# Giving turns and sums the score banks, maxima a ring of their own, and two earlier seams: one core, 32 groups of heads

## The reference: two transformer layers, of which the second layer's cross attention matters most

```python
x = x + _L0_xattn_ref(_layernorm(x), ctx, Wq, bq, Wk, bk)          # softmax over the width
x = x + _L0_ffn_ref(_layernorm(x), gate_w, gate_proj, up_proj, down_proj)   # 8 experts, top 2 of a router
x = x + _L1_xattn_ref(_layernorm(x), ctx, pos, pos, Wq, Wkv, Wout, bout)    # 32 heads of 16, rotary positions
x = x + _L1_ffn_ref(_layernorm(x), Wg, Wu, Wd, Wr, Ag, Bg, Au, Bu, Ad, Bd)

# in _L0_ffn_ref
router_logits = x_flat @ gate_w.T
top_w, sel = jax.lax.top_k(router_logits, TOPK)

# in _L1_xattn_ref
logits = jnp.einsum('bqhd,bkhd->bhqk', q, k) * scale
w = jax.nn.softmax(logits, axis=-1)
attn = jnp.einsum('bhqk,bkhd->bqhd', w, v)
```

## Time and profile before

| what | value |
|---|---|
| median of 3 runs | 1711.52 us (1708.54 to 1712.14) |
| profiled execution: its time, its span | 1712.57 us, 1710.9 us |
| PE, DVE, ACT, POOL busy | 1599.5, 1066.7, 782.0, 457.6 us |
| mean granted TensorE clock | 0.962 |
| router loop | about 160 to 187 us |
| second attention, 32 groups | 645.9 to 1004 us |

### The profile page before, as it was taken

One profiled execution on the slowest core, in us unless ns is written; L12 is line 12 of the kernel. 1 busy time (PEld: TensorE's weight loads), 2 busy tenths in 40 slices (PEclk: granted clock), 3 DMA queues, 4 the chain that ended last, 5 costly groups with the idle time before them and its releaser, 6 DMA issues. The chain is left out here.

```text
span 1710.9 us, 25136 instructions
## 1 busy us (share of the span) xinstructions
PE 1599.5 (93%) x8556; PEld 1173.2 (69%) x8556; DVE 1066.7 (62%) x1959; ACT 782.0 (46%) x1239; POOL 457.6 (27%) x422
## 2 busy tenths in 40 slices
PE   6987789999968989999999989999999999999998
PEld 5776679999957754333333357668888888888886
DVE  5876733222238887999999936655555557545456
ACT  5653323333325526888888853443333333223232
POOL 1120023332227861111210002233233323333332
PEclk8999789999988987999999999989999999999999
DMA  8996126654255764332222212443423345422221
GB/s 276 340 348 243 58 81 225 240 214 151 69 182 181 246 180 111 76 76 76 68 73 69 58 20 98 147 128 130 132 83 133 112 160 228 166 77 77 79 68 50
DMA packets 110364, 236.40 MB, mean 138 GB/s; under 512 B 39888, under 2 KB 53840, under 8 KB 101536
## 3 DMA queue, kind: packets, MB, share of 16 engines
q1 hardware_dynamic: 104000, 214.33, 37.6%
q0 software_dynamic: 6240, 20.45, 3.6%
HBM read 274.84 MB, written 93.45 MB: 215 GB/s over the span
## 5 line engine op out<-in xcount | busy, mean ns | idle before, releaser
L1319 DVE TENSOR_REDUCE early_top<-r_ring 128x1 f32<-128x512 f32 x480 | 304.2, 681 | 16.7 <-PE r_ring L1330 9.2
L2057 ACT ACTIVATE r_probs<-r_st 128x1024 f32<-128x1024 f32 x256 | 251.4, 1023 | 50.6 <-PE r_st L1959 50.3
L48 PE MATMUL f_bank<-late_xnT,late_weights 128*128 128x512 f32 x1056 | 252.4, 391 | 0.0
L48 PEld LDWEIGHTS f_bank<-late_xnT,late_weights 128*128 128x128 f32 x1056 | 196.6, 188 | 41.1 <-issue 0.7
L2855 DVE TENSOR_TENSOR attn<-attn,f_bank 128x512 f32<-128x512 f32 x132 | 90.8, 688 | 195.0 <-PE f_bank L48 130.7
L48 PE MATMUL m_bank<-w_place,m_xT 128*128 x936 | 167.2, 328 | 3.0 <-DVE m_xT L1220 3.0
L2849 ACT ACTIVATE attn<-f_bank 128x512 f32<-128x512 f32 x132 | 78.9, 598 | 179.9 <-PE f_bank L56 125.5
L48 PEld LDWEIGHTS m_bank<-w_place,m_xT 128*128 128x128 f32 x936 | 152.6, 190 | 6.9 <-issue 3.6
L1988 PE MATMUL r_out<-r_probs,early_v 128*17 128x512 f32 x1024 | 136.5, 605 | 0.1
L56 PE MATMUL f_bank<-late_am,late_weights 128*128 128x512 f32 x528 | 135.6, 392 | 0.3 <-DVE attn L2855 0.3
L3060 POOL TENSOR_TENSOR wout_split<-attn,wout_split 128x512 fp32r<-128x512 f32 x66 | 85.6, 1297 | 187.0 <-ACT wout_split L3036 187.0
(11 more groups left out here) (330 smaller groups left out, 2782.3 us busy)
## 6 DMA issues: line engine op xcount, KB each, us to landing
w_place<-expert_split SPq DMA_DIRECT2D x72, 1408.0 KB
w_place<-expert_split SPq DMA_DIRECT2D x36, 1024.0 KB
late_w_dram<-late_weights SPq DMA_DIRECT2D x11, 1920.0 KB, 8.2
expert_split<-w_place SPq DMA_DIRECT2D x10, 1408.0 KB
w_place<-expert_split SPq DMA_DIRECT2D x36, 384.0 KB
late_weights<-late_w_dram SPq DMA_DIRECT2D x11, 1024.0 KB, 5.2
late_weights<-late_w_dram SPq DMA_DIRECT2D x11, 896.0 KB, 4.8
early_slots<-y_rows SPq DMA_DIRECT2D x16, 512.0 KB, 6.5
```

The source lines that it names most:

```text
L48: last = nc.tensor.matmul(out, l, r, start=(i == 0), stop=(i == len(passes) - 1))
L1319: return nc.vector.reduce_max(self.top[g % 2][:, q, h:h + 1], bank[:], AXIS_X)
L2057: nc.scalar.activation(probs[k][:, 2 * pair:2 * pair + 2, :], st_ps[pair][:], ACT.Exp, scale=SCALE).then_inc(exp_done, 1)
```

## The change: who uses which bank, the order of a group, and the work around two seams

1. **Attention banks.** The ring of three holds maxima alone. The two turns go into the first bank of `st_ps[1]` (`turn_ps`). To leave it free for them, scores (1, 1) go into `st_ps[0]`, so that `st_ps[0]` carries five of a group's eight pairs and `st_ps[1]` three.
2. **Order of a group** on TensorE and ScalarE, and VectorE's inversion one maximum later in the group (after the first of q = 3).
3. **Seam into the attention.** The second group's 16 maxima go round seven banks, 12 spare products in place of 8, no wait for the last stores at the block's end (SP and POOL wait later, where the data is used).
4. **Front seam and router.** Statistics, deviation and inverse of tiles 0 to 11 move into the last batch of `phase_attention0`; those of tiles 12 to 15 into the router loop. VectorE normalises three tiles ahead, `xT` has a third place (`third`, in `hT`), the router's weights are turned after tile 1, constants are set behind the loop, and the load of three expert weights waits for tile 10.

```diff
-        PLACES = KT * GROUP + 2
-        SHIFT_PLACE, OUT_PLACE = 4, 8
...
+        turn_ps = st_ps[1][:, 0, :]
+
+        def score_bank(k, pair):
+            return st_ps[0 if (k, pair) == (1, 1) else pair]
+
+        def ring(g, q, h):
+
+            return ring_ps[((g - early.AHEAD) * KT * GROUP + q * GROUP + h) % 3]
...
+            def bank_free(g, q, h):
+
+                wait_count(pe, max_read, (g - AHEAD) * KT * GROUP + q * GROUP + h - 2)
...
-                wait_count(pe, exp_done, (g * KT + k) * 2 + pair - 1)
+                if (k, pair) == (2, 1):
+                    pe.wait_ge(sums_copied, g) if g else pe.wait_ge(shift_copied, 1)
+                else:
+                    wait_count(pe, exp_done, (g * KT + k) * 2 + pair - (0 if (k, pair) in ((1, 1), (2, 0)) else 1))
...
                 wait_count(pe, shift_made, g + 1 - AHEAD)
-                bank_free(g + 1, SHIFT_PLACE)
-                early.turn_shift(nc, g, ring(SHIFT_PLACE), ident).then_inc(shift_turned, 1)
+                pe.wait_ge(exp_done, 2 * KT * (g - 1) + 2)
+                early.turn_shift(nc, g, turn_ps, ident).then_inc(shift_turned, 1)
...
                 pe.wait_ge(out_copied, g + 1)
-                bank_free(g + 3, OUT_PLACE)
+                if g + 2 < GROUPS:
+                    pe.wait_ge(shift_copied, g + 2)
...
-            first_maxima(12, 8)
+            first_maxima(12, 5)
             turn_first_shift()
-            first_maxima(20, 12)
-            spare_products(nc, 8, qk_ps[0][1], wv[:, HI, 0, 0:P], wv[:, HI, 1, :])
+            first_maxima(17, 15)
+            pe.wait_ge(shift_copied, 1)
+            spare_products(nc, 12, shift_ps, wv[:, HI, 0, 0:P], wv[:, HI, 1, :])
...
-            for i in range(RING):
-                sp.wait_ge(qk_out[i], STORES * DMA * len(range(i, PAIRS, RING)))
...
+            for i in range(3):
+                normed_rows(i)
+            for i in range(TILES):
+                lo_x(i)
...
+                if i == 2:
+                    token_moments(nc, n, range(TILES - TPB, TILES))
+                    token_var(nc, n, LATE_TILES)
+                if i == TPB + 2:
+                    token_rstd(nc, dve, n, LATE_TILES, 2)
+                if i + 3 < TILES:
+                    normed_rows(i + 3)
```

More of the change, by code:

```diff
@@ L583, in _ @@
                     prep(b, 3 + t)
+                    if not ahead and t == TPB - 2:
+                        token_std(nc, act, norm, EARLY_TILES, 1)
         @block.vector
@@ L680, in _ @@
                 for t in range(1, TPB):
+                    if not ahead:
+                        token_moments(nc, norm, range((t - 1) * TPB, t * TPB))
+                        if t == TPB - 1:
+                            token_var(nc, norm, EARLY_TILES)
                     add(b, t)
@@ L872, in _ @@
             sp.dma_start(gw_raw, io["L0_ffn_gate_w"]).then_inc(gw_in, DMA)
-            for unit in range(3 * (E0 - 1), weights.UNITS):
-                weights.load(sp, unit)
             for i in range(TILES):
+                sp.wait_ge(n.xn_ready, i + 1)
+                if i == TILES - XN:
+                    for unit in range(3 * (E0 - 1), weights.UNITS):
+                        weights.load(sp, unit)
                 sp.wait_ge(n.xn_ready, i + 1)
@@ L1310, in __init__, with pairs_stored @@
         self.ones_set = ctx.enter_context(nc.semaphore("early_ones_set"))
+        self.qk_out = [ctx.enter_context(nc.semaphore(f"early_qk_out{i}")) for i in range(self.QK_RING)]
+    def pairs_stored(self, engine, pairs):
+        for i, out in enumerate(self.qk_out):
+            engine.wait_ge(out, self.QK_STORES * DMA * len(range(i, pairs, self.QK_RING)))
     def set_ones(self, engine, kM, done, each=lambda done: None):
@@ L2078, in _, with read_maxima @@
         def _(dve):
-            def read_maxima(g, q):
-                for h in range(GROUP):
+            def read_maxima(g, q, heads):
+                for h in heads:
                     dve.wait_ge(max_ready, ((g - AHEAD) * KT + q) * GROUP + h + 1)
-                    early.read_maximum(nc, g, q, h, ring(place(q, h))).then_inc(max_read, 1)
+                    early.read_maximum(nc, g, q, h, ring(g, q, h)).then_inc(max_read, 1)
             def make_shifts(g):
```

209 lines of the change are left out of this document (105 added, 104 removed).

## The result

The changed kernel takes 1702.33 us (median of 13 runs, 1697.33 to 1708.10) against 1711.95 us for the kernel before (13 runs beside it, 1705.93 to 1715.56): a ratio of 0.9946, 95% interval 0.9934 to 0.9959, so 9.2 us less (7.0 to 11.3). Forecast were 22.2 us less. The profiled execution has a span of 1701.7 us against 1710.9, the same 9.2.

| stretch | before | after | difference | forecast |
|---|---|---|---|---|
| start to the last `add` of the first phase | 152.24 | 154.34 | +2.1 | 0 |
| to the logits' copy behind the router loop | 35.36 | 30.68 | -4.7 | -3.1 |
| to the first of the first two groups' maxima | 426.17 | 429.41 | +3.2 | 0 |
| to the attention's first exponentials | 33.38 | 32.77 | -0.6 | -1.3 |
| first group | 14.96 | 10.48 | -4.5 | -4.0 |

The account below looks back on a forecast made before the run. VectorE was taken to bound the attention, with 0.78 us of waits a group above a 10.28 us floor. Attention 14.8, tail −1.0, seam 1.3, clock 4.0 and front 3.1 gave 22.2 us less: 1689.3 us, range 1681 to 1700.

Parts of the forecast that it names:

- the main mechanism: Attention: VectorE's waits for a late TensorE shrink, period 11.06 to 10.55 us over 29 periods, 14.8 us less.
- nothing took their place through `st_ps[0]`: Answers an attention rival: returns through that bank replace the ring's waits, period 11.6, 1724 us; chance 4%.
- Values by themselves cost 0.18 us of starving: Attention: values directly between two maxima, as k=0 between (1, 2) and (1, 3), make VectorE wait 0.18 us.
- 0.03 lost: Attention: values k=1 between maxima (3, 0) and (3, 1), where the moved inversion gives 0.16 more, cost 0.03 us.
- The floor of 10.28 stays: VectorE's instructions are the same.: Attention: VectorE's least time per group, from reads, inversion and shifts, is unchanged by the change at 10.28 us.
- The tail: Last two attention groups, without maxima and paced by ScalarE: 1.0 us more, bounds 0.5 and 1.5.
- the seam: Into the attention: phase starts 0.8 us earlier, or 1.3 if the clock returns in the spare products.
- The front: First tiles' normalisation and router loop: 3.1 us less, bounds 1.5 and 4.5.
- only 0.6 is left: Front: first tile is normalised 2.05 us earlier, but at the router's third product 0.6 us of that remains.
- The clock's return: First attention group: twelve spare products bring back full clock, about 11 us for 14.96, 4.0 less; a little likelier than not.
- VectorE is full: Attention rival: VectorE has no waits to lose, only front, seam and tail count, 3 us less, 1708.6 us; chance 7%.
- only the turns' waits go: Attention rival: each of four values costs VectorE 0.13 us, period 10.80, 1697 to 1702 us; chance 12%.

Follow-up runs that it names:

- e9: e5 with the values of key tiles 0 and 1 done for only 256 of 512 columns, two key tiles' sums dropped; 1688.12 us, ratio 0.9867.
- e4: The changed kernel with POOL's splitting of the output weight held until VectorE has made that group's shifts; 1701.53 us, ratio 0.9933.
- e5: e4 with 192 unused bytes per partition behind the normalisation tensors, shifting the expert stage's buffers; 1699.05 us, ratio 0.9915.
- e8: e4 with 8 spare products in place of 12 at the attention's seam; 1701.21 us, ratio 0.9936.
- e11: e10 with no spare products at the attention's seam; 1698.63 us, ratio 0.9937.
- e10: e5 with 8 spare products in place of 12 at the attention's seam; 1698.90 us, ratio 0.9931.
- e14: e10 with a pad of 448 bytes in place of 192, buffers 256 bytes off their place; 1695.52 us in one run.

## Why the prediction was wrong

The sign and the main mechanism were right: the turns' waits went, nothing took their place through `st_ps[0]` (ScalarE's waits before exponentials are 1.9 us a group, near the 2 forecast), and 0.27 of the 0.51 us a group came. It failed in size, in these steps:

- *"Values by themselves cost 0.18 us of starving"* at (1, 2) and *"0.03 lost"* at (3, 0). They cost 0.28 and 0.13, with 0.07 in place of 0.05 at k=3: 0.48 in place of 0.27 (forecast with its roundings), period 10.79 in place of 10.55, 29 x 0.24 = **7.0 us**. The mis-sized term is the 0.33 us from a maximum's start to the values', worked out from a row with a turn in it; it is 0.42 here (757.70 to 758.12). With it the step gives 0.54 + 0.42 + 0.98 + 0.73 = 2.67 against four reads of 2.40, which is 0.27. For (3, 0) the same 0.27 less the inversion's 0.16 is 0.11. e9 shows both: with shorter values both waits are gone, and the period is 10.42.
- *"The floor of 10.28 stays: VectorE's instructions are the same."* They are, but the moved inversion moved POOL's division 0.6 us later, and POOL's split behind it, onto VectorE's shift, in the four periods that became long: 1.5 us (e4), with the open 0.3 of group 19 **1.8 us**. The prediction counted what the move gave VectorE and not what is queued behind it on POOL.
- Part 4 moved the normalisation's tensors ahead and every buffer of the expert stage by 320 bytes: **1.7 us** (e5). No step of the prediction had it.
- The tail cost 1.4 in place of 1.0, inside its bounds, and the seam gave 0.6 in place of 1.3. TensorE was not through with its maxima at 639.5 but at 640.98, which is 640.3 in the times of the kernel before (the stretch starts 0.66 us later here), and the twelve products behind them took 4.73. Together **1.1 us**.
- The front gave 4.7 us in place of 3.1. Counted from the last `add`, the router's third product starts at 13.0 us (14.3 before), so 1.3 were left of the earlier start where the prediction has *"only 0.6 is left"*, and the sixteenth at 28.7 (33.3 before). So the 13 tiles gave 3.4 in place of 2.5. From one logits' turn to the next the pace is 1.28 a tile, as forecast (1.27), but over all 13 tiles it is 1.21.
- The clock's return gave 4.5 in this profile (forecast 4.0), but that was luck of this profile. Of the eleven profiles with this order and without SP's wait (twelve, eight or no spare products), one has a first group of 10.48 us, eight have 11.86 to 12.00 and two 14.1: 3 us is the fair figure. The reason given, longer dense work, is not borne out (e8, e11).
- 2.1 us at the start and 1.5 between the experts and the first maxima are left. The executions differ in both places. From the last expert tile's copy to the first maximum it is 125.8 to 128.8 us over the eighteen profiles, 127.0 before and 128.5 in the changed kernel. In the first phase's last batch TensorE ran at 0.50 for 3.4 us after 2.2 us of idling that is there before too. The same 24 products before and after, and the window:

```profile
138.74 5.74 PE L48 MATMUL a_mm<-w_place 128*128 128x512 f32 x24 [2.22 <-DVE w_place L589]
...
139.25 7.34 PE L48 MATMUL a_mm<-w_place 128*128 128x512 f32 x24 [2.22 <-DVE w_place L595]
```

```profile
138.99:142.40 3.41, 3.15 (x8) 2.48 (x9) 0.20 (x1) 0.00 (x0) 0.00 (x0) 0.57 1.05 365
```

Twelve of the fifteen profiles with part 4 have this, none of the three without. It costs 1.6 us here, yet the last `add` comes at 152.5 to 155.5 us in the twelve and at 152.2 to 153.5 in the others; whether part 4 brings it about or the phase's place in time, no run here tells.

7.0 + 1.8 + 1.7 + 1.1 + 3.6 - 1.6 - 0.5 is 13.1, which is the miss between 22.2 and 9.2 but for roundings.

The rival *VectorE is full* has fallen: VectorE did a group in 10.42 us in e9, where 0.68 for each of 16 reads with inversion and shifts would want 11.5. The period of *only the turns' waits go* (10.80) is what came, by 0.41 us at two values and not by 0.13 at each of four. That rival's time, up to 1702 us, is also next to the 1702.33 measured, but partly by luck: it too lacks the 1.7 and 1.8 us.

## What to carry over

Before an operation is moved to spare a wait, follow its consumer on the other engine to what is queued behind it: here 0.6 us later on POOL held VectorE for 0.45 us and made four periods 0.35 us longer, which a mean over all groups hides. Price a block between two tiles of a ring from the start of the last tile ahead of it, in the very sequence that the new order makes; in this ring of three a maximum could come 0.5 us late, by the estimate that the measured waits bear out, and what was beyond it came back at each such place in every group. When a buffer is allocated earlier, compare the pace of every later stage that the diff does not touch; e5, e10 and e11, with the pad and POOL's split held back, have the lowest medians of the complete kernels timed more than once here (1698.6 to 1699.1 us), though their intervals meet that of the changed one.

## What the runs showed of the hardware that was not expected

- Moving the expert stage's buffers in SBUF by 64 or 128 bytes (modulo 256) makes its tiles 0.7% longer (6.745 and 6.750 us against 6.700), moving them by 256 (e14) does nothing. The products that read xT start 1.4 ns further apart. That it is TensorE's reading of its operands, and not another engine's use of the same buffers, is argued from this and not shown.
- POOL's subtraction of two operands held VectorE's 0.18 us scalar instruction for 0.45 us, and no reduction.
- A maximum and a score product, which use 48 and 50 rows, start together (756.42 and 756.43 us) and last 0.49 us each. The Trainium skill ("TensorE: Matmul & The Clock Gate", section "Why this matters for your kernels") says that products of few rows in different row groups run at the same time; the trace agrees.
- The clock came back to 1.00 in the first group after 4 us of an idle TensorE (at 650.0 in e11), and fell to 0.50 again after twelve spare products (652.1 to 655.5 in e4) as after eight (644.0 to 654.2 in e10).
